# A state space layer on one core: paired scans, states put in by TensorE, two side banks, convolution on ScalarE and GpSimd

## What is computed

```python
xz = xs @ in_proj_w.T                       # 384 -> 2 x 768
xin, z = jnp.split(xz, 2, axis=-1)
xc = depthwise_conv(xin, conv_w)            # 4 taps along the tokens
xin = silu(xc + conv_b)
dt, Bm, Cm = split(xin @ x_proj_w.T)        # 24, 16, 16
dt = softplus(dt @ dt_proj_w.T + dt_proj_b)
A = -exp(A_log)
def step(h_prev, inp):                      # over 2304 tokens
    x_t, dt_t, B_t, C_t = inp
    dA = exp(dt_t[..., None] * A)
    dBx = dt_t[..., None] * B_t[:, None, :] * x_t[..., None]
    h_new = dA * h_prev + dBx               # 768 channels x 16 states
    y_t = einsum('bds,bs->bd', h_new, C_t)
    return h_new, y_t
y = (ys + xin * D) * silu(z)
out = layernorm(y @ out_proj_w.T)
```

## Time and profile before

| | us |
|---|---|
| median of 3 timed runs | 6280.98 |
| lowest, highest | 6262.24, 6282.42 |
| the profiled execution's own time | 6270.08 |
| its span | 6268.3 |
| mean granted clock of TensorE (share of full speed) | 0.927 |

### The profile page before, as it was taken

The page is one execution under the profiler, slowest core; times in us unless marked ns, Lnnn a source line. Parts: engine busy times, 40 slices in busy tenths (PEclk is TensorE's granted clock), DMA queues, the critical chain, the costliest instruction groups (busy, mean ns, idle before and its releaser), DMA issues.

```text
span 6268.3 us, 78225 instructions
## 1 busy us (share of the span) xinstructions
PE 5086.3 (81%) x28644; PEld 3933.0 (63%) x28644; DVE 4781.1 (76%) x6523; ACT 2805.0 (45%) x4858; POOL 2379.9 (38%) x2894
## 2 busy tenths in 40 slices
...
DVE  3999999999999999999999997637373753333333
...
PEclk8999999999999999999999998788888898999999
...
GB/s 67 1 16 23 8 8 8 8 16 23 8 8 8 8 16 23 8 8 8 8 8 8 8 5 37 0 32 12 35 12 35 12 54 26 31 31 23 31 31 20
DMA packets 73548, 115.49 MB, mean 18 GB/s; under 512 B 4132, under 2 KB 70208, under 8 KB 73164
## 3 DMA queue, kind: packets, MB, share of 16 engines
...
...
## 4 chain that ended last, share of the span: by engine, by line
PE 44%; DVE 28%; issue 16%; ACT 8%; POOL 3%; DMA 0%; SPq 0%; DVEq 0%; ACTq 0%; POOLq 0%
DVE a_h L720 13%; PE pw L1606 7%; DVE a_acc L734 7%; PE ps L1573 6%; PE pw L436 5%; PE ps L347 4%; PE ps L428 3%; PE ps L971 2%; PE ps L387 2%; ACT a_dA L561 2%; PE pw L1573 2%; POOL b_xw L1450 2%; PE ps L1059 2%; PE pw L1059 2%; PE ps L1015 1%
## 5 line engine op out<-in xcount | busy, mean ns | idle before, releaser
L720 DVE TENSOR_TENSOR_SCAN a_h<-a_dA,a_st,ps 128x384 f32<-128x384 f32 x1920 | 1861.8, 997 | 77.1 <-PE ps L428 74.3
L561 ACT ACTIVATE a_dA<-a_dt,a_Aneg 128x384 f32<-128x384 f32 x2304 | 1320.2, 607 | 481.8 <-DVE a_h L720 475.6
L824 POOL TENSOR_SCALAR a_dBT<-a_dtxT,a_BC 128x768 f32<-128x768 f32 x1152 | 1057.8, 936 | 818.9 <-PE ps L428 817.8
L428 PEld LDWEIGHTS ps<-g_ident,a_dBT 128*128 128x128 f32 x6912 | 885.5, 146 | 734.8 <-DVE a_h L720 328.4
L428 PE MATMUL ps<-g_ident,a_dBT 128*128 128x128 f32 x6912 | 1191.4, 285 | 181.3 <-DVE a_h L720 171.5
L436 PE MATMUL pw<-g_ident,a_h 128*128 128x128 f32 x6912 | 1023.0, 289 | 122.6 <-DVE a_h L720 120.6
L734 DVE SCALAR_TENSOR_TENSOR a_acc<-pw,a_BC,a_acc 128x768 f32<-128x768 f32 x1080 | 1070.4, 991 | 33.1 <-PE pw L436 32.3
L436 PEld LDWEIGHTS pw<-g_ident,a_h 128*128 128x128 f32 x6912 | 835.7, 149 | 188.2 <-DVE a_h L720 179.7
L1714 DVE TENSOR_TENSOR d_hf<-d_hf,ps 128x384 f32<-128x384 f32 x288 | 159.1, 554 | 560.3 <-ACT d_hf L1644 553.0
L387 PE MATMUL ps<-a_xn,a_WinT 128*128 128x384 f32 x864 | 380.8, 527 | 91.9 <-DVE a_dt L625 41.5
L327 PE MATMUL ps<-a_WoT,a_sz 128*128 128x384 f32 x864 | 362.8, 504 | 73.7 <-ACT a_ob L448 68.1
...
## 6 DMA issues: line engine op xcount, KB each, us to landing
a_xs<-in_x SPq DMA_DIRECT2D x24, 576.0 KB, 3.9
x<-a_xs SPq DMA_DIRECT2D x24, 576.0 KB, 3.0
b_x<-x SPq DMA_DIRECT2D x24, 576.0 KB, 4.4
e_xs<-x SPq DMA_DIRECT2D x24, 576.0 KB, 3.8
out<-e_xs SPq DMA_DIRECT2D x24, 576.0 KB, 3.0
a_sx<-in_x SPq DMA_DIRECT2D x19, 576.0 KB, 3.9
x<-b_x SPq DMA_DIRECT2D x16, 576.0 KB, 3.1
...
```

The costliest lines, as they stand in the source:

```text
L428: t = e.transpose(m[f"ps{idx % 3}"][:, tb * 128:(tb + 1) * 128], m[f"a_dBT{g % 2}"][:, tb, c * 128:(c + 1) * 128], ident[:])
L561: e.activation(m[f"a_dA{idx % NDA}"][:], m[f"a_dt{k % 2}"][:, c, :], ACT.Exp, scale=m["a_Aneg"][:, c, n:n + 1]).then_inc(s["a_exp"], 1)
L720: e.tensor_tensor_scan(m[f"a_h{g % 2}"][:, c, :], m[f"a_dA{idx % NDA}"][:], m[f"ps{idx % 3}"][:, 0:T], 0.0 if q == 0 else m["a_st"][:, c, ...
L824: t = e.tensor_scalar(m[f"a_dBT{g % 2}"][:, tb, :], m[f"a_dtxT{o}"][:, tb, :], m[f"a_BC{o}"][:, tb, n:n + 1], 1.0, ALU.mult, ALU.mult)
```

## The change

It touches only the state space layer.

1. Two channel tiles are scanned by one instruction of 2 x (384 + 1) columns. In front of each tile stands an extra column: its decay (column 0 of a_dA) is 0, and its input is the initial state, which TensorE writes by a matmul of the identity with two columns of a_st (or of a tile of zeros) into PSUM. The pair lies in one double bank (pw0, pw1) at columns 126 to 895, with both extra columns in the lower bank. a_dA has 5 buffers of a pair instead of 12 of one tile; LEAD is 7.
2. PSUM is divided anew: pw0 and pw1 hold inputs, pw2 alone the turned states (one buffer in place of two), ps2 and ps3 are two side banks with a `Turn` of their own: D, X, G and the statistics on ps2, the rest on ps3.
3. Main steps alternate: inputs and scan on even steps, turning and weighting on odd ones, three pairs behind the scans, across the border of chunks. a_acc has two buffers. D moves to steps 7 to 14. TensorE takes its side work only before even steps (`every=2`).
4. All six tiles are convolved by ScalarE and GpSimd.
5. Statistics are loaded in pieces of one channel tile, 18 for an image, through one buffer.

The diff, cut to its core:

```diff
+PAIRS = STEPS // 2
+COL = 511 - (T + 1)
-LEAD = 8
-NDA = 12
+LEAD = 7
+NDA = 5
-POOL_CONV = (0, 2, 3, 5)
-DVE_CONV = (1, 4)
-A_AT = (0, 2, 3, 5, 6, 8)
+A_AT = (7, 8, 10, 11, 13, 14)
...
-        due(n)
+        if n % every == 0:
+            due(n)
...
+    def inputs(k, p):
+        pi, q = PAIRS * k + p, k % NQ
+        g, c = NS * k + p // 3, 2 * (p % 3)
+        ps = m[f"pw{pi % 2}"]
+        w.wait_ge("p_dbt", g + 1)
+        w.wait_ge("v_scan", pi - 1)
+        if q > 0:
+            w.wait_ge("p_st", g - NS + 1)
+        first = m["a_st"][:, c:c + 2, p // 3] if q > 0 else m["a_zero"][:]
+        for h in range(2):
+            for tb in range(TB):
+                at = COL + h * (T + 1) + 1 + tb * 128
+                e.transpose(ps[:, at:at + 128], m[f"a_dBT{g % 2}"][:, tb, (c + h) * 128:(c + h + 1) * 128], ident[:])
+        e.matmul(ps[:, COL:COL + T + 2:T + 1], ident[:], first, start=True, stop=True, skip_group_check=True).then_inc(s["pe_b"], 1)
+    def turned(hh):
+        g, tb = divmod(hh, TB)
+        w.wait_ge("v_scan", 3 * g + 3)
+        w.wait_ge("v_acc", hh)
+        for c in range(6):
+            t = e.transpose(m["pw2"][:, c * 128:(c + 1) * 128], m[f"a_h{g % 2}"][:, c, 1 + tb * 128:1 + (tb + 1) * 128], ident[:])
+        t.then_inc(s["pe_h"], 1)
...
+            if n % 2 == 0:
+                inputs(k, n // 2)
+            elif PAIRS * k + n // 2 >= TB:
+                turned(PAIRS * k + n // 2 - TB)
+        march(side, STEPS, main, every=2)
+    for i in range(TB):
+        turned(PAIRS * NCH - TB + i)
...
+            w.wait_ge("v_scan", idx // 2 - NDA + 1)
+            e.activation(m[f"a_dA{idx // 2 % NDA}"][:, idx % 2, 1:T + 1], m[f"a_dt{k % 2}"][:, c, :], ACT.Exp, scale=m["a_Aneg"][:, c, n:n + 1]).then_inc(s["a_exp"], 1)
...
+    def scan(k, p):
+        pi, g, c = PAIRS * k + p, NS * k + p // 3, 2 * (p % 3)
+        w.wait_ge("pe_b", pi + 1)
+        w.wait_ge("a_exp", 2 * pi + 2)
+        w.wait_ge("pe_h", 3 * (g - 1))
+        w.wait_ge("p_st", g - 1)
+        e.tensor_tensor_scan(m[f"a_h{g % 2}"][:, c:c + 2, :].rearrange("p c t -> p (c t)"), m[f"a_dA{pi % NDA}"][:].rearrange("p c t -> p (c t)"),
+                             m[f"pw{pi % 2}"][:, COL:COL + 2 * (T + 1)], 0.0, ALU.mult, ALU.add).then_inc(s["v_scan"], 1)
...
-    for u, i in enumerate(POOL_CONV):
+    for i in range(6):
         yield 12 + 3 * i
...
-        w.wait_ge("p_sz", 6 * (k - 1))
+        w.wait_ge("p_sz", 6 * (k - 2) + i + 1)
...
-    def stats(b, q):
-        w.wait_ge("v_st", GN * (b - 1) + 18 if q == 0 else GN * b + 3 * q)
-        e.dma_start(m["a_sx"][:], xv[b, :, :, q * T:(q + 1) * T]).then_inc(s["d_sx"], 16)
+    def stats(b, i):
+        q, c = divmod(i, 3)
+        w.wait_ge("v_st", GN * (b - 1) + 18 if i == 0 else GN * b + i)
+        e.dma_start(m["a_sx"][:], xv[b, :, c, q * T:(q + 1) * T]).then_inc(s["d_sx"], 16)
...
+        more = 3 * NQ if q == 2 and b + 1 < NB else 0
+        for i in range(more - 5):
+            stats(b + 1, i)
         if k > 0:
             store0(e, m, d, w, k - 1)
         if k + 2 < NCH:
             load(k + 2)
+        for i in range(max(0, more - 5), more):
+            stats(b + 1, i)
```

More of the change, by code:

```diff
@@ L82, in step, with march @@
         self.at = next(self.gen, None)
-def march(gens, steps, main=None, scale=1.0):
+def march(gens, steps, main=None, scale=1.0, every=1):
     side = [Paced(g) for g in gens]
@@ L140, in place @@
     m = Memory(nc, ctx)
-    for i in range(4):
-        m.t[f"ps{i}"] = ctx.enter_context(nc.psum_tensor(f"ps{i}", [128, 512], F32))
+    for i in range(3):
+        m.t[f"pw{i}"] = ctx.enter_context(nc.psum_tensor(f"pw{i}", [128, 1024], F32))
     for i in range(2):
-        m.t[f"pw{i}"] = ctx.enter_context(nc.psum_tensor(f"pw{i}", [128, 1024], F32))
+        m.t[f"ps{i}"] = m["pw2"][:, 512 * i:512 * i + 512]
+        m.t[f"ps{i + 2}"] = ctx.enter_context(nc.psum_tensor(f"ps{i + 2}", [128, 512], F32))
     m.section(nc.sbuf_base)
@@ L160, in place @@
     m.new("a_xn", [128, 3, T])
-    m.new("a_sx", [128, 3, T])
+    m.new("a_sx", [128, T])
     m.new("a_dt0", [128, 6, T])
@@ L164, in place @@
     m.new("a_xs0", [128, 3, T])
-    m.new("a_dtl", [64, T])
     m.new("a_dt3", [128, T], F32R)
+    for i in range(NTM):
+        m.new(f"a_tm{i}", [128, T])
     early = m.at
@@ L169, in place @@
     m.new("a_one", [128, 1])
+    m.new("a_zero", [128, 2])
     m.new("a_xs1", [128, 3, T])
@@ L184, in place @@
     for i in range(NDA):
-        m.new(f"a_dA{i}", [128, T])
+        m.new(f"a_dA{i}", [128, 2, T + 1])
     for i in range(2):
-        m.new(f"a_h{i}", [128, 6, T])
+        m.new(f"a_h{i}", [128, 6, T + 1])
     m.new("a_st", [128, 6, NS])
@@ L194, in place @@
     m.new("a_pc", [128, 3, 2])
-    m.new("a_acc", [128, TB, DI])
+    for i in range(2):
+        m.new(f"a_acc{i}", [128, TB, DI])
     m.new("a_ob", [128, TB, C])
@@ L199, in place @@
     m.new("a_lsc", [128, TB, 2])
-    for i in range(NTM):
-        m.new(f"a_tm{i}", [128, T])
     m.section(late)
@@ L351, in pre_pe @@
         if j == 0:
-            S.claim("v_dt3", k + 1)
+            D.claim("v_dt3", k + 1)
             w.wait_ge("a_xi", k + 1)
             w.wait_ge("d_w0", 96)
-        t = e.matmul(ps[:, 0:T], m["a_WxT"][:, j, :], m[f"a_xin{o}"][:, j, :], start=j == 0, stop=j == 5)
+        t = e.matmul(pd[:, 0:T], m["a_WxT"][:, j, :], m[f"a_xin{o}"][:, j, :], start=j == 0, stop=j == 5)
     t.then_inc(s["pe_X"], 1)
@@ L439, in l0_pe @@
-        march(side, STEPS + 3, main)
+            if n % 2 == 0:
[5 more added lines that the diff above has]
+        turned(PAIRS * NCH - TB + i)
 def post_act(e, m, w, k):
@@ L456, in pre_act @@
     s, o, ps, pv = m.s, k % 2, m["ps3"], m["a_pv"]
-    raw, xs = m["a_raw"], m[f"a_xs{k % 3}"]
+    pd, raw, xs = m["ps2"], m["a_raw"], m[f"a_xs{k % 3}"]
     yield 1
@@ L467, in pre_act @@
         e.activation(raw[:, i, 3:T + 3], ps[:, 0:T], ACT.Copy).then_inc(s["a_raw"], 1)
[L468 to L479 removed]
+        w.wait_ge("d_w0", 96)
+        w.wait_ge("p_halo", k + 1)
+        w.wait_ge("a_raw", 6 * k + i + 1)
+        w.wait_ge("pe_BC", k)
+        for j in range(1, 4):
+            yield 11 + 3 * i + j
+            pr = 18 * k + 3 * i + j - 1
+            if pr >= NTM:
+                kb, rb = divmod(pr - NTM, 18)
+                w.wait_ge("p_cv", 24 * kb + 4 * (rb // 3) + rb % 3 + 2)
+            e.activation(m[f"a_tm{pr % NTM}"][:], raw[:, i, j:j + T], ACT.Copy, scale=pv[:, i, j:j + 1]).then_inc(s["a_pr"], 1)
     yield 37
[L481 to L482 removed]
+    w.wait_ge("p_cv", 24 * (k + 1))
     e.activation(m[f"a_xin{o}"][:], m[f"a_xin{o}"][:], ACT.Silu).then_inc(s["a_xi"], 1)
@@ L605, in pre_dve @@
 def pre_dve(e, m, w, k):
[L606 removed]
+    s, o, ps, pv, raw = m.s, k % 2, m["ps2"], m["a_pv"], m["a_raw"]
     xin, dt, dt3 = m[f"a_xin{o}"], m[f"a_dt{o}"], m["a_dt3"]
[L608 to L621 removed]
     yield 51
@@ L710, in main @@
         def main(n):
[L711 to L736 removed]
+            if n % 2 == 0:
+                scan(k, n // 2)
+            elif PAIRS * k + n // 2 >= TB:
+                weighed(PAIRS * k + n // 2 - TB)
+        march(side, STEPS, main)
+    for i in range(TB):
+        weighed(PAIRS * NCH - TB + i)
 def post_pool(e, m, w, k):
```

201 lines of the change are left out of this document (71 added, 130 removed).

## The result

The changed kernel takes 6203.15 us (median of 4 runs, 6177.74 to 6207.28), the kernel before 6281.13 (4 runs). The ratio is 0.9884, 95% interval 0.9863 to 0.9904: faster by 78 us, or 1.2%. Forecast were 6075 us, a gain of 206 on that median. The sign and the wide range (5880 to 6220) held, but the gain was well under half of the forecast one. The profiled execution took 6206.49 us, 63.6 under that of before.

A forecast was written before the change was run, and what follows sets the result against it. VectorE, in the state space layer, was taken to set the pace. Gains of 173, 136 and 161 us and losses of 138, 115 and 22 gave -195, from 6270.1 to 6075 us; 8-in-10 range 5880 to 6220.

The forecast's parts named there:

- Part 1: VectorE's scans: two channel tiles in one scan, 1.65 us a pair from start to start, 173 us gained.
- The one-pass reading: Alternative for the long scan, not taken: one pass (396 ns) and 541 fixed, a gain of 633 us.
- Part 2: Convolution taken off VectorE: 5.9 us a chunk, 136 us gained.
- Part 3: Pipelining across chunks, two accumulators, two side banks: all 7.0 us of idle time a chunk could go, 161 us gained.
- Part 4: Convolution onto GpSimd: 36.7 us of work in steps 12 to 30 against VectorE's 24.0; 6 us a chunk, 138 lost.
- Part 5: TensorE: one turning buffer, side work only every second step; stalls of 5 us a chunk, 115 us lost.
- the nine meetings: Side matmuls sharing a bank, outside part 4's stall: one Z and BC, three V, one Z, four T; 0.55 us each.
- A: Rival: leads on GpSimd and TensorE absorb two thirds of parts 4 and 5; 5907 us, chance 0.22.
- B: Rival: the long scan on VectorE saves little, 0 to 60 us instead of 173; 6190 to 6250 us, chance 0.11.
- D: Rival: slower by TensorE's clock, decisive below a mean of 0.85 in the layer; 6390 us at 0.80, chance 0.12.
- C: Rival: no net change, B and twice part 5 together; 6252 to 6290 us, chance 0.05.
- What the prediction said of ScalarE: Six more scaled copies a chunk, and decays 7 tiles ahead in 10 buffers instead of 8 in 12, cost nothing.

The follow-up runs named there:

- experiment 3: Convolution of tiles 1 and 4 put back on VectorE, against the changed kernel: 6256.24 us, ratio 1.0008.
- the fastest kernel: Changed kernel with side work at every step, LEAD 5 for 7, four pairs of decay tiles for five, five a_tm buffers for three: 5994.85 us, ratio 0.9557.
- experiment 5: Four pairs of decay tiles for five: on every1 0.9948; with five a_tm buffers for three as well, on every1 0.9879, on the changed kernel 1.0029.
- experiment 6: LEAD 5 for 7: on the changed kernel 0.9848, on every1 0.9652, there with four decay pairs 0.9685, and with five a_tm buffers too 0.9557.
- experiments 1 and 7: 1: side work at every step instead of every second, on the changed kernel, ratio 0.9725; 7: back to every second step, on the fastest kernel, 0.9838.
- every1: Changed kernel with TensorE's side work let in at every step instead of every second: 6083.31 us, ratio 0.9725.
- experiment 8: Extra matmul that puts in the initial states left out: on the changed kernel 6123.32 us, ratio 0.9763; on the fastest kernel 5953.12 us, 0.9495.
- experiment 2: One third of the input, output and gate projections' matmuls left out, against the changed kernel: 6143.54 us, ratio 0.9824.

## Where the prediction held, and the step that failed

**Part 1 (two tiles in one scan) held.** A pair is 1753 ns long where 1.73 us was forecast, and 1.67 from start to start against 1.65. By the same count a scan of before took 0.917 with a state tile and 0.856 without. The gain is then (1.83 - 1.67) x 960 + (1.71 - 1.67) x 192 = 161 us against 173. The one-pass reading (633) is refuted. 1753 ns for 770 columns beside 937 for 384 is 2.1 ns for each further column, twice the 1.03 of the weighting. The Trainium skill, "DVE: opcode table, instruction layouts, handler registers and perf-mode slots", section "Datapath and trigger behaviour", has the built-in scan at half throughput, and the trace agrees.

**Part 2 (convolution) held** in VectorE's own time: L620 and L617 are gone. They were 5.2 us a chunk from start to start, though, not 5.9: the sum took their full durations, ends that lie under the next start included, so 120 us and not 136.

**Part 3 held in what it removed.** No wait stands at the end of a chunk, where 1.9 us did.

**Part 4 was too large and half of it the wrong chain.** It had 6 us a chunk; experiment 3 shows 2. GpSimd's work was counted rightly: in the fastest kernel the stretch of 36.7 runs from 1448.59 to 1485.13, 36.5 us. But the lead of a_dBT covers it (0.06 us before pair 18). The other chain that the text named, three buffers of a_tm, a_raw, the projection, the inputs of step 24, is real: 1.7 us stand before pair 12, which is step 24. Two more buffers take about half of that away in the changed kernel (experiment 5) and most of the 3.3 us with side work at every step (experiment 6).

**Part 5 is the step that failed.** It said that "two side matmuls of 384 columns (0.64) fit" into 0.85 us of slack. One takes 0.65 and two take 1.30: the two records of one matmul had been read as two matmuls. (The 14 small ones of the earlier trace rows are seven by the code, for the same reason, so 0.25 each; the two-column matmul of the change itself takes 0.15, where 0.12 was put.) By the text's own count TensorE then needs 0.72 + 0.66 + 0.12 + 1.30 = 2.8 us in a pair that lasts 2.56, before any hand-over, and 28 of the 48 pairs have two such matmuls ahead of their inputs (60 by the code in the input projections, the output and the gate). So late scans are not confined to the nine meetings: outside pairs 9 to 13 and the statistics the waits are 9.7 us a chunk, where part 5 had 5. The size given for a meeting was about right for those of the transposes T (0.6, 0.6, 0.4, 0.6 before pairs 39, 40, 42, 43, where 0.55 was forecast); the three of the dt projection cost 0.1 to 0.3.

What the runs show of the cause: two side jobs ahead of one pair's inputs, with the turning held back by one buffer behind them, cost 100 and 176 us against the same work spread over both gaps (experiments 1 and 7). TensorE's amount of work in a full pair stays, 0.22 to 0.26 us in every1's timeline, and 0.15 us of it a pair is worth 76 us (experiment 8). It is not the whole answer: 11.7 us less of it a chunk brought 1.7 (experiment 2).

**A term was missing: a late scan costs more than its wait.** A weighting followed at once by a scan takes 0.91 us, its last 0.08 lying under the scan; followed by a wait it takes all of its 0.99. In the changed kernel 444 of 877 weightings are followed by a wait, 22.8 a chunk or 1.8 us. The kernel before lost some of this too, behind its scans and its weightings; counted over both, instructions without an instruction close behind rose from 11 to 26 a chunk, so the change in it is 1.2 us. The forecast had no such term, because it had few late pairs.

**A second one, by contention.** The softplus sum (L631) takes 695 ns in the mean, 571 before. In the timeline of 1634 to 1640 us and before it:

```profile
1633.46 1.00 POOL L797 TENSOR_TENSOR a_raw<-a_dt,a_xin 128x384 f32<-128x384 f32 x1
1633.57 1.31 DVE L631 SCALAR_TENSOR_TENSOR a_dt<-a_raw,a_dt 128x384 f32<-128x384 f32 x1
```

The same operation takes 0.53 with GpSimd's product away. The one in each chunk that meets it so takes 1.31, and the six of a chunk together 0.6 to 0.7 us more than before.

**The sum.** By the starts of the scans a chunk went from 157.2 to 154.0 us (mean of chunks 1 to 22). In us a chunk:

| | forecast | measured |
|---|---|---|
| scans | -7.5 | -7.0 |
| convolution off VectorE | -5.9 | -5.2 |
| idle time, statistics included | +4.6 (-7.0 + 6 + 5 + 0.6) | +7.0 (6.6 to 13.6) |
| lost overlap | none | +1.2 |
| softplus sum | none | +0.6 |
| together | -8.8 | -3.4 by these terms, -3.2 by the scans |

In the idle time, part 4 was four us too large and part 5, with what low clock there is, some six too small, so each hid part of the other's error. The statistics came as forecast: 13.7 us in three loads, where 14 were put. 23 chunks at 3.2 are 73 us; the start of the layer lost 8 and its end 1.4, where 8 were forecast for both, and 64 are left between the two profiles.

**Rivals.** A would have needed under 4 us idle. B is refuted by the scan's length, D by the clock (0.98 in the stretch of the earlier trace rows); a low clock shows at times before pair 27, and step 51 in place of 53 removes the wait there. The time, 6203, lies where B would have put it, but for another reason, and that it lies inside the wide range is in part luck, as parts 4 and 5 erred in opposite directions. C's range did not follow from its own terms: B and another 115 us are 6305 to 6365, not 6252 to 6290. What the prediction said of ScalarE, "nothing", held for the amount of its work and was wrong about its place: lead and stock are worth 21 to 165 us in experiments 5 and 6.

**The gains don't add.** From the changed kernel, relieving the chains alone (lead and copies) brings 29 us, every step alone 100, both together 205. Each relieves what the other still holds back, so a small gain from one edit was no proof that its chain did not matter.

**Open.** No kernel here had a second turning buffer, so what the single one costs, apart from the two side jobs ahead of it, is not shown. How much of the wait before pair 27 is the low clock was not separated from the order of the work. The 0.5 to 0.6 us before pair 7 stayed in every kernel here, and its cause was not tested.
